# Attention over 2048 batches of 40 fields: one load of x for values and residual of two slots of four, and the shift by the maxima as four 64 by 64 matmuls

## The chip, the cores and the metric

The kernel runs on one core of one Trainium2 chip. The metric is the device time of one execution in microseconds (us); lower is better.

## The reference, cut to what matters

For each of 2048 batches there is x of 40 fields by 64 numbers. Queries, keys, values and a residual are each a projection of x to 128 outputs (4 heads of 32); softmax attention runs over the 40 fields of a batch, per head; the result is relu(attention + residual).

```python
q = (einsum('bfe,oe->bfo', x, Wq) + bq).reshape(B, F, H, D)   # k and v likewise; B=2048 F=40 H=4 D=32
att = einsum('bfhd,bghd->bhfg', q, k) / sqrt(64)
att = softmax(att, axis=-1)
out = einsum('bhfg,bghd->bfhd', att, v).reshape(B, F, H * D)
res = einsum('bfe,oe->bfo', x, Wr) + br
return relu(out + res)
```

## The kernel before

A step handles 8 batches: 4 slots of 2 members. There are 256 steps. Member 0 of a slot lies in partitions 0 to 39 of the working tiles and member 1 in partitions 64 to 103; the lower and the upper 64 rows of TensorE's array are used as separate row groups throughout. `xT` holds x transposed twice, once in partitions 0 to 63 in natural order of the batches, and once in partitions 64 to 127 in the order `ORDER`, in which some slots have their two members exchanged ("crossed").

The order of work on each engine is written out by hand and bound by semaphores. In group n, TensorE does in turn:

- `queries_and_keys(n)` (L382, L386): queries from the lower rows into bank 0 of `o_bank`, keys from the upper rows into bank 1, 320 columns each, float32. A float32 matmul appears in the trace as two passes, each with its own weight load.
- `scores(n-1)` (L402): 16 small matmuls (32 passes, 80 columns) on the four 64 by 64 quarters of the array.
- `attend(n-3)` (L461): 32 small matmuls (64 passes, 33 columns), again on the four quarters. It writes `o_bank`, so it waits until ScalarE (L227) and VectorE (L316) have copied queries and keys out (`copied`).
- `shift(n-2)` (L438): two bf16 matmuls of the full 128 by 128 array and 320 columns that subtract each query's maximum from the scores in `s_buf`: the diagonal matrices `m_diag` made by GpSimd, moved through `pick`, which is nonzero in a 64 by 40 block per member.
- `values_and_residual(n)`: two bias matmuls of 256 columns in bf16 (L419 lower rows, L424 upper rows), and then for each of the four slots one matmul in the lower rows (values, L429) and one in the upper rows (residual, L431), x as the stationary operand and a weight matrix of 128 columns moving. The lower rows write bank 0 of `vr_bank`, the upper rows bank 1.

ScalarE copies `vr_bank` to `rv` (L254), swaps maxima, takes the exponentials of `s_buf` (L247, waits for `shifted`) and the relu (L234). VectorE makes the keys (L316), the maxima (L321, L327 to L332), the reciprocals (L337) and the division (L343), whose `att_ready` lets the next `queries_and_keys` start. GpSimd does three things in each group: `diagonals(n-2)` (L179, needs VectorE's `m_split`), `query_columns(n)` (L195, two instructions) and `add_residual(n-4)` (L187). SyncE's queue loads x eight steps ahead and stores y.

## Time and profile before

| | |
|---|---|
| runs | 938.09 us median of 3 (936.63 to 940.19) |
| the profiled execution | 944.5 us, with a span of 942.4 us |
| granted TensorE clock | 0.995 |
| busy | PE 916.0, PEld 680.3, DVE 726.7, ACT 769.2, POOL 876.5 us |

PE is TensorE's matmuls, PEld its weight loads, DVE VectorE, ACT ScalarE, POOL GpSimd. Times are us from the start of the span unless marked ns. A matmul's start is recorded, its end is modelled and overlaps the next ones, so that a PE that counts as busy may be standing: starts are to be compared with starts. A row of the timeline gives the start of the first of a merged group and the time to the end of its last, so the start of the last is the row's end less the mean duration of one.

### The profile page before, as it was taken

The page shows a single profiled execution, that of the slowest core. Times are in us where ns is not written, and L with a number is a line of the kernel's source. Part 1 is how long each engine was busy: PE and PEld are TensorE (multiplying, and loading weights), DVE is VectorE, ACT ScalarE, POOL GpSimd, SP SyncE. Part 2 cuts the span into 40 slices and gives each one's busy share as a digit, 9 for nine tenths or more (in the row PEclk, how much of TensorE's full clock was granted, in tenths as well). Part 3 has the DMA queues.
Part 4 walks back from the last instruction along what each step waited for, and adds up shares of the span by engine and source line. Part 5 has one row for each costly group of instructions (what it writes and reads, how often), then busy time and mean ns, then how long its engine had stood idle before and what let it go on. Part 6 is the DMA issues. An engine that isn't in the chain of part 4 may idle for free.

```text
span 942.4 us, 68912 instructions
## 1 busy us (share of the span) xinstructions
PE 916.0 (97%) x30720; PEld 680.3 (72%) x30720; DVE 726.7 (77%) x2066; ACT 769.2 (82%) x1541; POOL 876.5 (93%) x1028
## 2 busy tenths in 40 slices
PE   6999999999999999999999999999999999999996
PEld 4777777777777777777777777777777777777774
DVE  6777777778777877777777777777778777777775
ACT  4888888888887888878888788887888888888885
POOL 3999999999998999989999999999999999999997
PEclk9999999999999999999999999999999999999997
DMA  4333333333333333333333333333333333333321
GB/s 117 100 108 109 108 115 110 109 110 115 108 107 105 109 109 108 110 104 107 116 108 110 108 109 114 112 109 102 115 109 109 114 105 116 109 109 106 108 77 65
DMA packets 67433, 101.20 MB, mean 107 GB/s; under 512 B 13632, under 2 KB 46656, under 8 KB 67136
## 3 DMA queue, kind: packets, MB, share of 16 engines
q1 hardware_dynamic: 66704, 96.65, 33.7%
q8 instruction: 239, 3.92, 1.8%
q14 instruction: 58, 0.48, 0.2%
q10 hardware_dynamic: 432, 0.15, 0.1%
HBM read 54.81 MB, written 41.94 MB: 103 GB/s over the span
## 4 chain that ended last, share of the span: by engine, by line
PE 97%; issue 2%; ACT 0%; DMA 0%; DVE 0%; POOL 0%; POOLq 0%; ACTq 0%
PE vr_bank L429 24%; PE o_bank L461 22%; PE s_buf L402 19%; PE o_bank L382 14%; PE s_buf L438 10%; PE vr_bank L419 6%; PE vr_bank L431 1%; DMA biases<-bias_in 0%; PE o_bank L386 0%; POOL y_sum L187 0%; ACT rv L254 0%; ACT y_rows L234 0%; POOLq L35 0%; ACT q_flat L227 0%; PE vr_bank L424 0%
## 5 line engine op out<-in xcount | busy, mean ns | idle before, releaser
L179 POOL TENSOR_TENSOR m_diag<-m_split,ident 128x640 bf16<-128x640 bf16 x256 | 322.2, 1258 | 49.7 <-DVE m_split L332 35.2
L187 POOL TENSOR_TENSOR y_sum<-rv,y_att 128x512 f32<-128x512 f32 x256 | 302.9, 1183 | 1.9 <-DVE y_att L343 1.9
L195 POOL TENSOR_SCALAR q_bd<-q_flat,consts 128x320 f32<-128x320 f32 x512 | 265.8, 532 | 10.8 <-DVE kT L316 10.8
L431 PE MATMUL vr_bank<-w_cols,xT 64*128 64x128 f32 x2048 | 270.9, 273 | 0.0
L429 PE MATMUL vr_bank<-w_cols,xT 64*128 64x128 f32 x2048 | 270.7, 273 | 0.0
L254 ACT ACTIVATE rv<-vr_bank 128x1024 f32<-128x1024 f32 x256 | 260.1, 1016 | 0.0
L321 DVE TRANSPOSE_TENSOR_REDUCE s_buf<-s_buf 128x20 f32<-128x640 f32 x256 | 221.5, 865 | 46.2 <-PE s_buf L402 46.2
L429 PEld LDWEIGHTS vr_bank<-w_cols,xT 64*128 64x128 f32 x2048 | 251.2, 190 | 0.0
L431 PEld LDWEIGHTS vr_bank<-w_cols,xT 64*128 64x128 f32 x2048 | 250.4, 189 | 0.0
L461 PE MATMUL o_bank<-rv,pT 64*40 64x33 f32 x16384 | 225.0, 202 | 10.3 <-issue 8.3
L402 PEld LDWEIGHTS s_buf<-q_bd,kT 64*40 64x40 f32 x8192 | 150.9, 112 | 116.0 <-issue 115.0
L316 DVE TENSOR_SCALAR kT<-o_bank,biases 128x320 f32<-128x320 f32 x256 | 141.0, 551 | 116.7 <-PE o_bank L386 116.7
L461 PEld LDWEIGHTS o_bank<-rv,pT 64*40 64x40 f32 x16384 | 190.3, 118 | 51.8 <-issue 14.6
L227 ACT ACTIVATE q_flat<-o_bank,biases 128x320 f32<-128x320 f32 x256 | 134.9, 527 | 89.9 <-PE o_bank L386 85.6
L402 PE MATMUL s_buf<-q_bd,kT 64*40 64x80 f32 x8192 | 199.9, 233 | 1.2 <-issue 0.5
L247 ACT ACTIVATE pT<-s_buf 128x640 f32<-128x640 f32 x256 | 180.1, 704 | 19.7 <-PE s_buf L438 14.1
L382 PE MATMUL o_bank<-xT,w_cols 64*128 64x320 f32 x512 | 180.6, 433 | 5.7 <-DMA xT<-xT_in 5.7
L343 DVE TENSOR_TENSOR y_att<-o_bank,r_sum 128x512 f32<-128x512 f32 x256 | 177.1, 692 | 9.1 <-DVE r_sum L337 0.3
L386 PE MATMUL o_bank<-xT,w_cols 64*128 64x320 f32 x512 | 180.6, 433 | 0.0
L234 ACT ACTIVATE y_rows<-y_sum 128x512 f32<-128x512 f32 x256 | 159.0, 622 | 2.4 <-POOL y_sum L187 2.4
L240 ACT COPY m_swap<-s_buf 32x20 f32<-32x20 f32 x512 | 85.5, 167 | 54.5 <-DVE s_buf L321 48.4
L438 PE MATMUL s_buf<-m_diag,pick 128*128 128x320 bf16 x512 | 114.2, 305 | 1.1 <-POOL m_diag L179 1.1
(33 smaller groups left out, 624.1 us busy)
## 6 DMA issues: line engine op xcount, KB each, us to landing
xT<-xT_in SPq DMA_DIRECT2D x512, 104.0 KB, 2.5
y<-y_rows SPq DMA_DIRECT2D x512, 80.0 KB
w_cols<-w_in SPq DMA_DIRECT2D x1, 128.0 KB, 2.2
vr_bias<-vr_bias_in ACTq DMA_DIRECT2D x1, 128.0 KB, 3.4
consts<-consts_in ACTq DMA_DIRECT2D x1, 20.0 KB, 2.0
biases<-bias_in ACTq DMA_DIRECT2D x1, 1.0 KB, 3.7
```

What stands on the lines that cost most here:

```text
L179: pool.tensor_tensor(m_diag[:], m_split[:, place % 2].unsqueeze(2).to_broadcast([P, BLOCKS, QUAD]), ident[:].unsqueeze(1).to_broadcast([P, ...
L187: pool.tensor_tensor(y_sum[:, n % 3].rearrange("r (a d) -> r a d", d=DIM), rv[:, place % 4, 1, :, 0:DIM], y_att[:, place % 2].rearrange("r ...
L195: pool.tensor_scalar(q_bd[:, place % 4, :, s], q_flat[:, place % 2].rearrange("d (b f) -> d b f", f=FIELDS), consts[:, C_HEAD + s:C_HEAD + ...
L254: nc.scalar.activation(rv[:, place % 4].rearrange("k t a v -> k (t a) v")[:, :, 0:DIM], vr_bank[:].rearrange("k t (a d) -> k (t a) d", d=DIM),
L321: nc.vector.tensor_reduce(m_part[place % 2].rearrange("k (t b) -> k t b", t=2), s_buf[place % 2][:, :, 0:TOK].rearrange("k t (b c) -> k t ...
L382: nc.tensor.matmul(o_bank[:, 0, 0:TOK], w_cols[0:HALF, 0], tokens(place, 0), start=True, stop=True)
L386: nc.tensor.matmul(o_bank[:, 1, 0:TOK], w_cols[HALF:P, 0], tokens(place, HALF), start=True, stop=True).then_inc(qk_made, 1)
L402: mm = nc.tensor.matmul(s_buf[place % 2][HALF * member:HALF * member + FIELDS, t, 2 * FIELDS * slot:2 * FIELDS * (slot + 1)], kT[rows, pla ...
L429: nc.tensor.matmul(vr_bank[:, 0, OUT * pair:OUT * (pair + 1)], xT[0:HALF, place % 8, cols], w_cols[0:HALF, 1], start=False, stop=True, ski ...
L431: mm = nc.tensor.matmul(vr_bank[:, 1, OUT * pair:OUT * (pair + 1)], xT[HALF:P, place % 8, cols], w_cols[HALF:P, 1], start=False, stop=True ...
L438: mm = nc.tensor.matmul(s_buf[place % 2][:, t, 0:TOK], pick[:].rearrange("k m f -> k (m f)"), m_diag[:, t * (BLOCKS // 2):(t + 1) * (BLOCK ...
L461: mm = nc.tensor.matmul(o_part[HALF * g:HALF * g + FIELDS, member, jj * HEADS + h], pT[HALF * member:HALF * (member + 1), place % 2, h // ...
```

## The change

Three things change in what TensorE does.

1. In `values_and_residual`, slots 0 and 1 are projected as before (values from the lower rows, residual from the upper rows), while slot 2 is loaded once in the lower rows and multiplied by both weight matrices in one matmul of 256 columns, and slot 3 likewise in the upper rows. Values then lie in blocks 0, 1, 2 and 7 of `rv` and residuals in blocks 3 to 6. `w_cols` gets a third matrix (Wr with Wv below it), the column of ones in `rv` is written for all 32 blocks, and the bias goes to blocks 0 and 2 of either half.
2. `shift` becomes four matmuls, one per member and bank half: 64 rows by 40 columns of `pick` as weights, 320 columns moving, each into its member's partitions.
3. In `attend`, the bank of `o_part` follows whether the slot is crossed (slots 0 and 1 now are in both members) in place of the member; the order of the quarters of the array stays.

```diff
--- before.py
+++ after.py
@@ -17,8 +17,12 @@
 PAD = SLOTS * PAIR
 REST = P - PAIR
 
-ORDER = [MEMBERS * slot + member for member in range(MEMBERS) for jj in range(2)
-         for slot in (2 * jj + member, 2 * jj + 1 - member)]
+
+CROSSED = 2
+
+ORDER = [MEMBERS * slot + (member ^ (slot < CROSSED)) for slot in range(SLOTS) for member in range(MEMBERS)]
+
+VALUES, RESIDUAL = (0, 1, 2, 7), 3
 BLOCKS = HEADS * SLOTS * FIELDS // QUAD
 VW = DIM + 1
 SCALE = float(EMB) ** -0.5
@@ -40,7 +44,7 @@
             return ctx.enter_context(nc.semaphore(name))
 
 
-        w_cols = sb("w_cols", [P, 2, OUT])
+        w_cols = sb("w_cols", [P, 3, OUT])
         biases = sb("biases", [P, 2])
         consts = sb("consts", [P, C_ALL])
         pick = sb("pick", [P, MEMBERS, HALF], BF16)
@@ -63,7 +67,7 @@
         q_bd = sb("q_bd", [P, 4, GROUP, 2, FIELDS])
         kT = sb("kT", [P, 4, TOK])
         pT = sb("pT", [P, 2, 2, TOK])
-        rv = sb("rv", [P, 4, 2, SLOTS * HEADS, VW])
+        rv = sb("rv", [P, 4, 2 * SLOTS * HEADS, VW])
         m_swap = sb("m_swap", [P, 2, BLOCKS])
         m_split = sb("m_split", [P, 2, BLOCKS], BF16)
         r_sum = sb("r_sum", [P, 2, 8])
@@ -184,7 +188,7 @@
                 pool.wait_ge(att_ready, n + 1)
                 if not before(n, 3):
                     pool.wait_ge(y_ready, n - 2)
-                pool.tensor_tensor(y_sum[:, n % 3].rearrange("r (a d) -> r a d", d=DIM), rv[:, place % 4, 1, :, 0:DIM],
+                pool.tensor_tensor(y_sum[:, n % 3].rearrange("r (a d) -> r a d", d=DIM), rv[:, place % 4, RESIDUAL * HEADS:(RESIDUAL + SLOTS) * HEADS, 0:DIM],
                                    y_att[:, place % 2].rearrange("r (a d) -> r a d", d=DIM),
                                    ALU.add).then_inc(sum_ready, 1)
 
@@ -217,8 +221,8 @@
             act.dma_start(biases[:], bias_in).then_inc(loaded, 16)
             act.wait_ge(loaded, LOADS)
             for i in range(4):
-                nc.scalar.copy(rv[:, i, 0, :, DIM:VW],
-                               consts[:, C_REAL:C_REAL + 1].unsqueeze(2).to_broadcast([P, SLOTS * HEADS, 1])).then_inc(prepared, 1)
+                nc.scalar.copy(rv[:, i, :, DIM:VW],
+                               consts[:, C_REAL:C_REAL + 1].unsqueeze(2).to_broadcast([P, 2 * SLOTS * HEADS, 1])).then_inc(prepared, 1)
 
             def queries(n, place):
                 act.wait_ge(qk_made, n + 1)
@@ -251,7 +255,7 @@
                 act.wait_ge(vr_made, n + 1)
                 if not before(n, 4):
                     act.wait_ge(sum_ready, n - 3)
-                nc.scalar.activation(rv[:, place % 4].rearrange("k t a v -> k (t a) v")[:, :, 0:DIM],
+                nc.scalar.activation(rv[:, place % 4, :, 0:DIM],
                                      vr_bank[:].rearrange("k t (a d) -> k (t a) d", d=DIM),
                                      ACT.Copy).then_inc(vr_ready, 1)
 
@@ -410,34 +414,45 @@
 
 
 
+                def blocks(half, first, step):
+                    return vr_bank[:, half].rearrange("r (a c) -> r a c", c=OUT)[:, first::step]
+
+                def project(half, pair, first, step, count):
+                    rows = slice(HALF * half, HALF * (half + 1))
+                    return nc.tensor.matmul(blocks(half, first, step)[:, 0:count],
+                                            xT[rows, place % 8, PAIR * pair:PAIR * pair + P],
+                                            w_cols[rows, 1:1 + count],
+                                            start=False, stop=True, skip_group_check=True)
+
                 if not before(n, 1):
                     pe.wait_ge(vr_ready, n)
                 else:
 
                     pe.wait_ge(prepared, PREPARED)
                     pe.wait_ge(set_up, SET_UP)
-                nc.tensor.matmul(vr_bank[:, 0, 0:2 * OUT], bias_pick[0:HALF], bias_rows[0:HALF].rearrange("r s c -> r (s c)"),
+                nc.tensor.matmul(blocks(0, 0, 2), bias_pick[0:HALF], bias_rows[0:HALF],
                                  start=True, stop=False, skip_group_check=True)
                 if exists(n + 1):
 
                     pe.wait_ge(x_loaded[(place + 1) % 8], 32 * turn_of(n + 1, place + 1, 8))
-                nc.tensor.matmul(vr_bank[:, 1].rearrange("r (m j c) -> r m j c", m=MEMBERS, j=2)[:, :, 1],
-                                 bias_pick[HALF:P], bias_rows[HALF:P],
+                nc.tensor.matmul(blocks(1, 0, 2), bias_pick[HALF:P], bias_rows[HALF:P],
                                  start=True, stop=False, skip_group_check=True)
-                for pair in range(SLOTS):
-                    cols = slice(PAIR * pair, PAIR * pair + P)
-                    nc.tensor.matmul(vr_bank[:, 0, OUT * pair:OUT * (pair + 1)], xT[0:HALF, place % 8, cols],
-                                     w_cols[0:HALF, 1], start=False, stop=True, skip_group_check=True)
-                    mm = nc.tensor.matmul(vr_bank[:, 1, OUT * pair:OUT * (pair + 1)], xT[HALF:P, place % 8, cols],
-                                          w_cols[HALF:P, 1], start=False, stop=True, skip_group_check=True)
+                for pair in range(CROSSED):
+                    project(0, pair, pair, 1, 1)
+                    project(1, pair, 1 + pair, 1, 1)
+                project(0, 2, 2, 1, 2)
+                mm = project(1, 3, 0, 3, 2)
                 mm.then_inc(vr_made, 1)
 
             def shift(n, place):
                 pe.wait_ge(diag_ready, n + 1)
                 for t in range(2):
-                    mm = nc.tensor.matmul(s_buf[place % 2][:, t, 0:TOK], pick[:].rearrange("k m f -> k (m f)"),
-                                          m_diag[:, t * (BLOCKS // 2):(t + 1) * (BLOCKS // 2)].rearrange("k b i -> k (b i)"),
-                                          start=False, stop=True, skip_group_check=True)
+                    for member in range(MEMBERS):
+                        rows = slice(HALF * member, HALF * (member + 1))
+                        mm = nc.tensor.matmul(s_buf[place % 2][HALF * member:HALF * member + FIELDS, t, 0:TOK],
+                                              pick[rows, member, 0:FIELDS],
+                                              m_diag[rows, t * (BLOCKS // 2):(t + 1) * (BLOCKS // 2)].rearrange("k b i -> k (b i)"),
+                                              start=False, stop=True, skip_group_check=True)
                 mm.then_inc(shifted, 1)
 
             def attend(n, place):
@@ -451,16 +466,15 @@
                     pe.wait_ge(p_ready, n + 1)
                 if not exists(n + 1):
                     pe.wait_ge(vr_ready, n + 1)
-                for jj in range(2):
+                for idx in range(2):
                     for h in range(HEADS):
-                        for low in range(2):
+                        for c, slot in ((0, CROSSED + idx), (1, idx)):
                             for member in range(MEMBERS):
-                                slot = 2 * jj + low
-                                g = member ^ low
+                                g = member ^ c
                                 at = (2 * slot + h % 2) * FIELDS
-                                mm = nc.tensor.matmul(o_part[HALF * g:HALF * g + FIELDS, member, jj * HEADS + h],
+                                mm = nc.tensor.matmul(o_part[HALF * g:HALF * g + FIELDS, c, idx * HEADS + h],
                                                       pT[HALF * member:HALF * (member + 1), place % 2, h // 2, at:at + FIELDS],
-                                                      rv[HALF * member:HALF * (member + 1), place % 4, 0, slot * HEADS + h],
+                                                      rv[HALF * member:HALF * (member + 1), place % 4, VALUES[slot] * HEADS + h],
                                                       start=True, stop=True, skip_group_check=True)
                 mm.then_inc(o_made, 1)
 
@@ -512,7 +526,8 @@
             xT[:, half, :, :, HALF * member:HALF * member + fields] = columns[:, :, order[member::2]]
     arrays = {
         "xT_in": xT.reshape(steps, P, PAD),
-        "w_in": np.ascontiguousarray(np.stack([np.concatenate([Wq.T, Wk.T]), np.concatenate([Wv.T, Wr.T])], 1)),
+        "w_in": np.ascontiguousarray(np.stack([np.concatenate([Wq.T, Wk.T]), np.concatenate([Wv.T, Wr.T]),
+                                               np.concatenate([Wr.T, Wv.T])], 1)),
         "bias_in": np.ascontiguousarray(np.stack([bq, bk], 1)),
         "vr_bias_in": np.ascontiguousarray(np.stack([bv, br])[None]),
         "consts_in": consts,
@@ -523,9 +538,10 @@
     args.append(nc.dram_tensor("y", (steps, 2, FIELDS, SLOTS * OUT), _mybir.dt.float32, kind="ExternalOutput").ap())
     attention_kernel(nc, *args)
     r = run_bass_kernel_spmd(nc, [arrays], core_ids=[0])
-    rows = r.results[0]["y"].reshape(steps, 2, FIELDS, MEMBERS, 2, OUT)
-    y = np.empty((steps, 2, 2, MEMBERS, FIELDS, OUT), np.float32)
-    for member in range(MEMBERS):
-        for low in range(2):
-            y[:, :, low, member] = rows[:, low ^ member, :, member].transpose(0, 2, 1, 3)
+    rows = r.results[0]["y"].reshape(steps, 2, FIELDS, SLOTS, OUT)
+    y = np.empty((steps, SLOTS, MEMBERS, FIELDS, OUT), np.float32)
+    for slot in range(SLOTS):
+        for member in range(MEMBERS):
+            crossed = slot < CROSSED
+            y[:, slot, member] = rows[:, member ^ crossed, :, slot + 2 if crossed else slot - 2]
     return y.reshape(batch, FIELDS, OUT)
```

## Rows read from the trace of the kernel before

**Rows 1.** The page, busy time of each engine

```profile
PE 916.0 (97%) x30720; PEld 680.3 (72%) x30720; DVE 726.7 (77%) x2066; ACT 769.2 (82%) x1541; POOL 876.5 (93%) x1028
```

**Rows 2.** The page, the chain that ended last, by engine

```profile
PE 97%; issue 2%; ACT 0%; DMA 0%; DVE 0%; POOL 0%; POOLq 0%; ACTq 0%
```

**Rows 3.** Timeline of one step: start, length, engine, line, count

```profile
316.38 0.43 PE L382 MATMUL o_bank<-xT,w_cols 64*128 64x320 f32 x1
...
316.49 1.26 POOL L179 TENSOR_TENSOR m_diag<-m_split,ident 128x640 bf16<-128x640 bf16 x1
316.74 0.76 PE L402 MATMUL s_buf<-q_bd,kT 64*40 64x80 f32 x32
...
316.86 0.55 DVE L316 TENSOR_SCALAR kT<-o_bank,biases 128x320 f32<-128x320 f32 x1 [0.45 <-PE o_bank L386]
...
317.47 0.82 PE L461 MATMUL o_bank<-rv,pT 64*40 64x33 f32 x64
...
318.22 0.45 PE L438 MATMUL s_buf<-m_diag,pick 128*128 128x320 bf16 x2
...
318.60 0.28 PE L419 MATMUL vr_bank<-bias_rows,bias_pick 64*128 64x256 bf16 x1
...
318.64 0.69 DVE L343 TENSOR_TENSOR y_att<-o_bank,r_sum 128x512 f32<-128x512 f32 x1
...
319.61 0.43 PE L382 MATMUL o_bank<-xT,w_cols 64*128 64x320 f32 x1
```

**Rows 4.** Timeline: the last passes of values and residual, then queries

```profile
319.39 0.27 PE L429 MATMUL vr_bank<-w_cols,xT 64*128 64x128 f32 x1
...
319.50 0.27 PE L429 MATMUL vr_bank<-w_cols,xT 64*128 64x128 f32 x1
...
319.88 0.43 PE L382 MATMUL o_bank<-xT,w_cols 64*128 64x320 f32 x1
```

**Rows 5.** The page, costliest groups: busy us, mean ns of one, idle before

```profile
L179 POOL TENSOR_TENSOR m_diag<-m_split,ident 128x640 bf16<-128x640 bf16 x256 | 322.2, 1258 | 49.7 <-DVE m_split L332 35.2
L187 POOL TENSOR_TENSOR y_sum<-rv,y_att 128x512 f32<-128x512 f32 x256 | 302.9, 1183 | 1.9 <-DVE y_att L343 1.9
L195 POOL TENSOR_SCALAR q_bd<-q_flat,consts 128x320 f32<-128x320 f32 x512 | 265.8, 532 | 10.8 <-DVE kT L316 10.8
...
L461 PE MATMUL o_bank<-rv,pT 64*40 64x33 f32 x16384 | 225.0, 202 | 10.3 <-issue 8.3
...
L402 PE MATMUL s_buf<-q_bd,kT 64*40 64x80 f32 x8192 | 199.9, 233 | 1.2 <-issue 0.5
...
L438 PE MATMUL s_buf<-m_diag,pick 128*128 128x320 bf16 x512 | 114.2, 305 | 1.1 <-POOL m_diag L179 1.1
```

**Rows 6.** Source view of the first bias matmul's weight load: duration, first and last start

```profile
L419 PEld LDWEIGHTS vr_bank<-bias_rows,bias_pick x256: 92/93/102, 8.5 to 927.2; 64*128 64x128 bf16 x128
```

**Rows 7.** Timeline of TensorE, three longer steps: the second piece of attend

```profile
284.02 0.76 PE L461 MATMUL o_bank<-rv,pT 64*40 64x33 f32 x58 [0.16 <-issue]
...
288.04 0.69 PE L461 MATMUL o_bank<-rv,pT 64*40 64x33 f32 x50 [0.22 <-issue]
...
292.06 0.61 PE L461 MATMUL o_bank<-rv,pT 64*40 64x33 f32 x42 [0.22 <-issue]
```

**Rows 8.** The page, DMA queues: packets, MB

```profile
q8 instruction: 239, 3.92, 1.8%
```

**Rows 9.** Timeline of GpSimd alone over one step

```profile
320.00 1.26 POOL L179 TENSOR_TENSOR m_diag<-m_split,ident 128x640 bf16<-128x640 bf16 x1
321.24 1.04 POOL L195 TENSOR_SCALAR q_bd<-q_flat,consts 128x320 f32<-128x320 f32 x2
322.24 1.19 POOL L187 TENSOR_TENSOR y_sum<-rv,y_att 128x512 f32<-128x512 f32 x1
323.50 1.26 POOL L179 TENSOR_TENSOR m_diag<-m_split,ident 128x640 bf16<-128x640 bf16 x1
```

**Rows 10.** Timeline of the first 14 us

```profile
8.54 0.37 PE L419 MATMUL vr_bank<-bias_rows,bias_pick 64*128 64x256 bf16 x1 [1.37 <-DVE pick L310]
```

## The prediction

> **What bounds the kernel now.** I read the page's busy times first: TensorE and GpSimd are both above 90% [rows 1]. The chain that ended last lies on TensorE for nearly all of the span [rows 2]. But a matmul's end is modelled, so the chain cannot say whether TensorE works or stands. For that I took one step of the timeline and compared starts [rows 3]. From queries to queries it is cut so:
>
> - second queries pass 316.38 to first score 316.74: 0.36 us, of which the 320 columns take 0.27 (the same two passes are 0.27 apart in [rows 4]). Some 0.09 us are a gap, where the array goes from 64-row, 128-column tiles to 64 by 40 ones.
> - scores, 316.74 to 317.47: 0.73. Attend starts 0.06 us after VectorE has ended its copy of the keys (316.86 + 0.55 = 317.41). So this piece is the wait for the copies; the last score started at 317.50 less 0.23 [rows 5], that is 317.27.
> - attend, 317.47 to 318.22: 0.75. Its last pass started at 318.29 less 0.20 [rows 5] = 318.09, and shift starts 0.13 later. A pass of 33 columns needs, at the 0.83 ns a column of the queries (0.27 us for 320), 0.03. Again 0.10 us of gap, here from 64 by 40 tiles to the full array.
> - shift, 318.22 to 318.60: 0.38. Its second matmul started at 318.67 less 0.305 [rows 5] = 318.36, so one takes 0.14, two take 0.28, and 0.10 is a gap again, from the full array to 64 by 128.
> - bias, values and residual, 318.60 to 319.61: 1.01.
>
> With the 0.27 between the two queries passes this is 3.50 us, all of it TensorE's order and one wait on the copies. The mean step is longer: the first bias loads run from 8.5 to 927.2 over 255 steps [rows 6], 3.60 each. The 0.10 of difference is not spread evenly: in a long step attend falls into two pieces, with 0.16 to 0.22 us of standing between them, by the modelled ends, that no semaphore explains [rows 7]. There are 61440 loads and matmuls [rows 1] in 239 packets of instructions [rows 8], 257 to a packet against 240 to a step; in three such steps 58, 50 and 42 passes stand behind the break [rows 7], 8 passes or 16 instructions fewer a step, as the border of a packet would move. I take these breaks for late instruction packets: about 255 x 0.10 = 26 us in all.
>
> The second engine matters as much. GpSimd's step is 1.24 from diagonals to query columns, 1.00 on to the residual sum, and 1.19 for that sum [rows 9]; neighbours on GpSimd overlap by 0.02 to 0.04 in the records. That is 3.43 less 0.04, so 3.39 us when nothing holds it. Its busy time gives 876.5 / 256 = 3.42 [rows 1], less that last overlap the same 3.39. GpSimd has 0.11 us of slack in a step of 3.50, no more.
>
> **The change part by part.**
>
> Shift. The two switches of shape around it become one: attend's quarters and the new shift's are the same 64 by 64 tiles, so the 0.10 gap between attend and shift [rows 3] should go. That such a gap is not there without a switch is seen between scores and attend only in part, since the copies cover it. I price it at 0.10; bounds are 0 (the gap belongs to the end of attend, whatever follows) and 0.12 (the whole distance from the last attend pass but 0.01). The gap before the bias matmuls stays, since a switch remains. The streaming itself: four matmuls of 320 columns in two pairs, each pair on two different quarters (lower rows to lower partitions, upper rows to upper partitions). If a pair runs at once it takes 0.14 and two take 0.28, as now. That quarters do run at once is in the scores: 32 passes whose first and last start are 0.53 us apart (316.74 to 317.27), 0.017 a pass, where one pass of 80 columns streams 0.067. That is four at a time. I take 0.28; the other bound is 4 x 0.14 = 0.56, that is 0.28 us a step more. The four weight loads of 40 columns instead of two of 128 lie under attend's last passes and under the first pair, and cost nothing; uncovered, the nearest load row is 93 ns [rows 6] once.
>
> In all that the trace shows, lower and upper rows never write one bank together: queries and keys, scores, attend and values all keep one row group to one bank. The new shift is the first place where a pair writes the same bank, in different partitions. Here the Trainium skill speaks against the change: TensorEngine Tiling (Array Packing), Gotcha 1: PSUM Pressure, says that different row tiles cannot access the same PSUM bank simultaneously. Its page PSUM — Partial Sum Buffer, section PSUM bank collisions raise a hardware error, narrows this: different column tiles may share a bank if their partitions are disjoint, which holds here. By the first the sum is that of the second rival below; by the second that of the forecast. No row of before shows the case.
>
> Values and residual. The columns are the same: 2 x 128 + 256 in each half in place of 4 x 128. A pass of 128 columns takes 0.111 (319.39, 319.50, 319.61), one of 320 takes 0.27 [rows 3, 4]; on the line between them 256 takes 0.217, against 0.222 for two of 128. Two float32 passes: 0.01 us a step saved. That two weight loads a step go away in each half saves nothing by itself, because the passes are already as long as their columns on that line; bounds 0 and 0.02. The bias matmuls keep 256 columns: 0.
>
> Attend. The same 64 passes on the same quarters in the same order, other banks: within a group of four, neighbours now share a bank in different partitions. I price it at 0, on the same ground as shift; the upper bound is attend at half its overlap, 0.75 more, which would go with the second rival.
>
> Around it. ScalarE's copy of `vr_bank` and GpSimd's sum keep their sizes. The division sends `att_ready` at about 319.33 + 0.06 = 319.39, and the next queries start at 319.61: 0.22 of cover, of which the change takes 0.11, so that wait stays hidden. `m_diag` is done at 316.49 + 1.26 = 317.75 and wanted at 318.22, then 0.10 earlier: hidden too, until GpSimd falls behind. The 64 KB more of weights and the wider column of ones lie before 8.54, where TensorE has waited 1.37 us for VectorE's bias [rows 10]: 0.
>
> **The sum.** TensorE: 3.50 - 0.10 - 0.01 = 3.39 a step. GpSimd: 3.39. They meet, so a gain beyond 0.11 cannot show. The breaks for instruction packets stay as they are, 236 instructions a step against 240. I take 0.105 a step for two engines so close together: 256 x 0.105 = 27 us. The profiled execution goes from a span of 942.4 to 915.5 and from 944.5 to 917.6; it lies 6.4 us above the median of the runs, and 938.09 - 27 = **911 us**.
>
> **The rivals.**
>
> 1. Forecast, 911: chance 0.70, own range 904 to 920 (the breaks may go by a third, 9 us, either way).
> 2. Pairs of the shift run one after the other, because two row groups write one bank. For it: no row shows such a pair at once, and every stage before keeps its row groups in banks of their own. Against: the partitions are disjoint, and quarters run four at a time in the scores. The tiling page of the Trainium skill, cited above, speaks for this rival. Price +0.28 - 0.11 = +0.17 a step, 44 us: 982 us, slower. It decides from the point where the second of a pair starts more than 0.055 us after the first (two pairs eat 0.11). Chance 0.12.
> 3. The change does little: the gap ahead of shift is attend's own tail and stays. Then only 0.01 a step, 3 us: 935; with half of the gap, 922. For it: attend's ends are modelled, and each gap in the trace stands at a change of stage as well as of shape. Against: the gap is 0.09 to 0.10 at three switches behind matmuls of 320, 33 and 320 columns alike. The Trainium skill, in TensorEngine Tiling (Array Packing), Key Properties, says that changing the tiling mode, and not merely the tile, drains the engine; by it the time is the forecast's. Chance 0.11, of which 0.03 at half.
> 4. The breaks in attend grow, as the same instructions are wanted in less time and the shift's loads and matmuls, four more instructions, stand right behind attend. A break of 0.3 in every third step instead of the present mean of 0.10 would be half again, +13 us: 924. Chance 0.07, of which 0.01 within 0.5% of before.
>
> A measurement of this kernel can tell about 0.5%, some 5 us. Faster by more: 0.70 + 0.06 + 0.03 = 0.79. Within: 0.08 + 0.01 = 0.09. Slower: 0.12. The range leaves out the second rival and little else: 903 to 936.
>
> **What would show it.** In a quiet step: shift starts under 0.05 us after the last attend pass, not 0.13; the two matmuls of a shift pair start together and the pairs 0.13 to 0.14 apart; from shift's start to the bias still 0.38; the 256-column passes 0.217 apart; the step 3.39 and GpSimd with no idle time before its diagonals. Wrong would be: shift pairs staggered by 0.13 (second rival), the gap ahead of shift still there (third), attend longer than 0.65 to its last start, or GpSimd's step above 3.39, with shift waiting on `m_diag`.

## The result, and the profile after

The changed kernel takes 924.84 us (median of 4 runs, 921.35 to 926.6) against 938.58 us before (median of 4): a ratio of 0.985, 95% interval [0.9814, 0.9886]. It is faster by 13.7 us where 27 were forecast. The interval leaves out 1, so the gain is real, though it is under 2%. A second comparison (run c0 below) gave 0.9846 [0.9826, 0.9866].

The profiled execution took 923.84 us with a span of 921.1. The page of the changed kernel, busy times, then the chain that ended last by engine, then the queue of TensorE's instructions:

```profile
PE 892.3 (97%) x30208; PEld 626.7 (68%) x30208; DVE 726.7 (79%) x2066; ACT 770.6 (84%) x1541; POOL 872.1 (95%) x1028
...
PE 93%; POOL 3%; issue 2%; DVE 1%; DMA 0%; ACT 0%; POOLq 0%; ACTq 0%
```

```profile
q8 instruction: 235, 3.85, 1.8%
```

236 loads and matmuls a step (60416 / 256) in place of 240, and GpSimd and VectorE now have pieces of the chain, where [rows 2] had none. One quiet step in the timeline answers to [rows 3]:

```profile
352.57 0.45 PE L386 MATMUL o_bank<-xT,w_cols 64*128 64x320 f32 x1
...
352.86 0.43 PE L386 MATMUL o_bank<-xT,w_cols 64*128 64x320 f32 x1
...
353.10 1.26 POOL L183 TENSOR_TENSOR m_diag<-m_split,ident 128x640 bf16<-128x640 bf16 x1
353.22 0.76 PE L406 MATMUL s_buf<-q_bd,kT 64*40 64x80 f32 x32
...
353.95 0.82 PE L475 MATMUL o_bank<-rv,pT 64*40 64x33 f32 x64
...
354.58 0.44 PE L452 MATMUL s_buf<-m_diag,pick 64*40 64x320 bf16 x4
...
354.95 0.28 PE L433 MATMUL vr_bank<-bias_rows,bias_pick 64*128 64x256 bf16 x1
...
355.07 1.04 PE L422 MATMUL vr_bank<-w_cols,xT 64*128 64x128 f32 x12
355.12 0.69 DVE L347 TENSOR_TENSOR y_att<-o_bank,r_sum 128x512 f32<-128x512 f32 x1
...
355.95 0.45 PE L386 MATMUL o_bank<-xT,w_cols 64*128 64x320 f32 x1
```

By starts: attend to shift 0.63 in place of 0.75, and the last attend pass (354.77 less 0.20 = 354.57) stands 0.01 ahead of the shift, not 0.13. Shift to bias 0.37, bias to queries 1.00 in place of 1.01. Together with 0.65 and 0.73 for the first two pieces this is 3.38 us, against 3.50. One thing is new: the first queries pass takes 0.29 instead of 0.27. Another step shows the shift's pairs at once:

```profile
319.31 0.32 PE L452 MATMUL s_buf<-m_diag,pick 64*40 64x320 bf16 x2
319.34 0.21 PE L475 MATMUL o_bank<-rv,pT 64*40 64x33 f32 x2
319.45 0.32 PE L452 MATMUL s_buf<-m_diag,pick 64*40 64x320 bf16 x2
```

The two matmuls of a pair are one row of the timeline, the next pair follows 0.14 later, and the shift starts while attend's last passes are still going in. GpSimd alone:

```profile
349.70 1.27 POOL L183 TENSOR_TENSOR m_diag<-m_split,ident 128x640 bf16<-128x640 bf16 x1
...
353.10 1.26 POOL L183 TENSOR_TENSOR m_diag<-m_split,ident 128x640 bf16<-128x640 bf16 x1
...
356.47 1.27 POOL L183 TENSOR_TENSOR m_diag<-m_split,ident 128x640 bf16<-128x640 bf16 x1
```

3.40 and 3.37 apart: GpSimd runs without idle time here. In the whole trace 135 of its steps have no idle time, and they take 3.384 us at the median. The first of the next two rows, from the view of waits (us in total, times, longest), is one that the kernel before did not have at all, the queries' weight load waiting for the division. The second says that GpSimd still waits for VectorE 91 times, as it did 92 times before:

```profile
PEld o_bank L386 <- DVE y_att L347: 35.4, 214, 0.3
POOL m_diag L183 <- DVE m_split L336: 30.1, 91, 1.6
```

So a quiet step came out as forecast. The mean step did not. The first bias loads (source view, to be read as [rows 6]) give (906.5 - 8.7) / 255 = 3.52, and the long steps are there as before, with the break in attend:

```profile
L433 PEld LDWEIGHTS vr_bank<-bias_rows,bias_pick x256: 92/92/99, 8.7 to 906.5; 64*128 64x128 bf16 x128
```

```profile
326.65 0.46 PE L475 MATMUL o_bank<-rv,pT 64*40 64x33 f32 x26 [0.33 <-issue]
```

### The profile page after: what moved, and what is told of

Read it like the earlier page. It is cut to its first block, busy times and chain, and to the rows that moved or that the text cites. A ratio compares the mean times of both kernels' runs of the same rounds, so it can differ in the third digit from the quotient of the medians.

```text
span 921.1 us, 67888 instructions
## 1 busy us (share of the span) xinstructions
PE 892.3 (97%) x30208; PEld 626.7 (68%) x30208; DVE 726.7 (79%) x2066; ACT 770.6 (84%) x1541; POOL 872.1 (95%) x1028
## 3 DMA queue, kind: packets, MB, share of 16 engines
q8 instruction: 235, 3.85, 1.8%
## 4 chain that ended last, share of the span: by engine, by line
PE 93%; POOL 3%; issue 2%; DVE 1%; DMA 0%; ACT 0%; POOLq 0%; ACTq 0%
PE vr_bank L422 24%; PE o_bank L475 22%; PE s_buf L406 19%; PE o_bank L386 15%; PE s_buf L452 7%; PE vr_bank L433 6%; POOL y_sum L191 1%; POOL m_diag L183 1%; POOL q_bd L199 1%; PE o_bank L390 0%; DMA biases<-bias_in 0%; ACT y_rows L238 0%; POOLq L39 0%; DVE s_buf L325 0%; PE vr_bank L438 0%
## 5 line engine op out<-in xcount | busy, mean ns | idle before, releaser
L422 PE MATMUL vr_bank<-w_cols,xT 64*128 64x128 f32 (+1 forms) x3072 | 269.0, 308 | 0.1
L475 PE MATMUL o_bank<-rv,pT 64*40 64x33 f32 x16384 | 229.6, 202 | 12.1 <-issue 8.4
L475 PEld LDWEIGHTS o_bank<-rv,pT 64*40 64x40 f32 x16384 | 192.9, 117 | 54.4 <-issue 17.9
L422 PEld LDWEIGHTS vr_bank<-w_cols,xT 64*128 64x128 f32 x3072 | 195.2, 190 | 0.2 <-issue 0.2
L386 PE MATMUL o_bank<-xT,w_cols 64*128 64x320 f32 x512 | 186.8, 445 | 5.7 <-DMA xT<-xT_in 5.7
L390 PE MATMUL o_bank<-xT,w_cols 64*128 64x320 f32 x512 | 187.5, 446 | 0.0
L452 PE MATMUL s_buf<-m_diag,pick 64*40 64x320 bf16 x1024 | 114.9, 297 | 2.0 <-POOL m_diag L183 1.6
L386 PEld LDWEIGHTS o_bank<-xT,w_cols 64*128 64x128 f32 x512 | 76.6, 186 | 45.7 <-DVE y_att L347 35.4
L336 DVE TENSOR_TENSOR m_split<-s_buf,m_split 32x20 bf16<-32x20 f32 x512 | 88.5, 173 | 16.6
```

Of the source, the lines that this page charges most:

```text
L386: nc.tensor.matmul(o_bank[:, 0, 0:TOK], w_cols[0:HALF, 0], tokens(place, 0), start=True, stop=True)
L390: nc.tensor.matmul(o_bank[:, 1, 0:TOK], w_cols[HALF:P, 0], tokens(place, HALF), start=True, stop=True).then_inc(qk_made, 1)
L422: return nc.tensor.matmul(blocks(half, first, step)[:, 0:count], xT[rows, place % 8, PAIR * pair:PAIR * pair + P], w_cols[rows, 1:1 + coun ...
L452: mm = nc.tensor.matmul(s_buf[place % 2][HALF * member:HALF * member + FIELDS, t, 0:TOK], pick[rows, member, 0:FIELDS], m_diag[rows, t * ( ...
L475: mm = nc.tensor.matmul(o_part[HALF * g:HALF * g + FIELDS, c, idx * HEADS + h], pT[HALF * member:HALF * (member + 1), place % 2, h // 2, a ...
```

## The experiments

All numbers of steps in this table come from the starts of the first queries matmul in each of the last 250 groups of TensorE's timeline. A step counts as quiet if it is within 0.06 us of the fastest fiftieth; the quiet column is the mean of those, "long" the number of the others, "breaks" the mean step less the quiet one. "Packet" is the time that 256 instructions take at the quiet pace, quiet x 256 / N, with N the loads and matmuls of a step. Ratios are to the kernel before on the same chip, which took 941.6 us beside c0 to e3, 942.1 beside e4 to e7 and 936.8 beside e8 to e11 (medians). Where e4 to e11 are set against c0, two ratios from different chips are subtracted, so a difference is known to some 3 or 4 us only.

| kernel | N | quiet | long | breaks | mean step | packet | ratio, 95% |
|---|---|---|---|---|---|---|---|
| before | 240 | 3.502 | 92 | 0.098 | 3.601 | 3.74 | 1 |
| changed | 236 | 3.387 | 117 | 0.131 | 3.518 | 3.67 | 0.985 [0.9814, 0.9886] |
| c0, changed again | 236 | 3.386 | 122 | 0.151 | 3.537 | 3.67 | 0.9846 [0.9826, 0.9866] |
| e1, shift only | 244 | 3.395 | 155 | 0.194 | 3.589 | 3.56 | 1.0058 [1.0032, 1.0083] |
| e2, projection only | 232 | 3.487 | 52 | 0.055 | 3.542 | 3.85 | 0.9878 [0.9857, 0.9898] |
| e3, one more switch | 234 | 3.474 | 74 | 0.080 | 3.554 | 3.80 | 0.988 [0.9858, 0.9902] |
| e4, half division | 236 | 3.370 | 103 | 0.137 | 3.507 | 3.66 | 0.9791 [0.9768, 0.9813] |
| e5, short sum | 236 | 3.385 | 104 | 0.119 | 3.505 | 3.67 | 0.9803 [0.9777, 0.9829] |
| e6, both | 236 | 3.370 | 98 | 0.137 | 3.507 | 3.66 | 0.9815 [0.9792, 0.9838] |
| e7, 256 instructions | 256 | 3.466 | 213 | 0.356 | 3.823 | 3.47 | 1.0584 [1.0559, 1.0609] |
| e8, the same, moved | 256 | 3.468 | 160 | 0.257 | 3.726 | 3.47 | 1.0416 [1.0371, 1.0461] |
| e9, four more | 240 | 3.393 | 114 | 0.152 | 3.545 | 3.62 | 0.9913 [0.9879, 0.9946] |
| e10, light stores | 236 | 3.387 | 86 | 0.107 | 3.494 | 3.67 | 0.9733 [0.9695, 0.9772] |
| e11, no bias | 233 | 3.385 | 124 | 0.127 | 3.513 | 3.72 | 0.9838 [0.9795, 0.9881] |

In e11 the profile lists 232 loads and matmuls a step, but its breaks keep one place in the packet only if 233 instructions a step are counted. That the further one is a wait, since two waits now stand ahead of one matmul, is inferred from the edit.

**c0 and the two parts.** c0 is the changed kernel unedited. e1 is the kernel before with one edit:

```diff
-                    mm = nc.tensor.matmul(s_buf[place % 2][:, t, 0:TOK], pick[:].rearrange("k m f -> k (m f)"), ...)
+                    for member in range(MEMBERS):
+                        rows = slice(HALF * member, HALF * (member + 1))
+                        mm = nc.tensor.matmul(s_buf[place % 2][HALF * member:HALF * member + FIELDS, t, 0:TOK],
+                                              pick[rows, member, 0:FIELDS], ...)
```

e2 is the changed kernel with that edit undone.

> The changed kernel once more, on the chip on which its parts run. Theory A (the time of a step is what its starts show: 3.41 us in a quiet step in place of 3.50, and breaks for instruction packets that vary from execution to execution): ratio 0.98 to 0.99, a spread of some 5 us. Theory B (the first ratio was too small by chance, and the gain is the 21 us between the two profiled spans): 0.975 to 0.98.

> The kernel before with only the shift changed. Theory A (the gap ahead of shift is the change of the array's shape): attend's start to shift's start 0.64 in place of 0.75, queries 0.66 in place of 0.63 because they now wait for the division, projection unchanged at 1.01; step 3.42, ratio about 0.987, nearly all of the change's gain. Rival (the gain comes from the fewer loads of the projection, or from the banks of attend): step above 3.48, ratio above 0.995.

> The changed kernel with the old shift of two full matmuls, so the new projection and attend's new banks alone. Theory A: projection 1.00 in place of 1.01, attend to shift 0.75 as before, step 3.49, ratio 0.995 to 1.00. Rival (fewer loads matter): ratio below 0.993.

c0's ratio was that of theory A, which puts the smaller gain of the first comparison down to more than chance. The stages of the two parts were as expected: e1's attend to shift 0.64 and its quiet step 3.395, e2's projection 1.00 and its quiet step 3.487. The times were the other way about: the shift alone, which brings 0.107 us a quiet step, made the kernel 0.6% slower, and the projection alone, which brings 0.015, made it 1.2% faster. What changed with them is the number of instructions (244 and 232) and with it the breaks. The view of waits for e1, then for e2, attend's loads that waited for nothing the profile shows:

```profile
PEld o_bank L464 <- issue: 24.9, 73, 1.1
```

```profile
PEld o_bank L472 <- issue: 7.8, 23, 1.1
```

My theory A had the ratios of both wrong: it priced the step by its quiet form. "Fewer loads matter", the rival for e2, was right in its number and not in its place: the projection became only 0.01 shorter.

**Is the gap the switch of shape?** e3 does the shift's first half in quarters and its second half as one full matmul.

```diff
-                for t in range(2):
-                    for member in range(MEMBERS):
...
+                for member in range(MEMBERS):
+                    ... (t = 0, as in the changed kernel)
+                mm = nc.tensor.matmul(s_buf[place % 2][:, 1, 0:TOK], pick[:].rearrange("k m f -> k (m f)"), ...)
```

> The changed kernel in which the shift's first half is done in quarters and the second half by one matmul of the full array: the same columns, one more change of shape, in the middle of the shift. Theory A (each change of shape costs 0.10 us): shift to bias 0.47 in place of 0.37, attend to shift still 0.64, step 3.48 to 3.50, ratio about 1.00. Rival (the gap is attend's tail, whatever follows, and four matmuls merely hide it): shift to bias stays at 0.37 to 0.39 and the time that of the changed kernel.

Timeline of e3:

```profile
400.92 0.82 PE L477 MATMUL o_bank<-rv,pT 64*40 64x33 f32 x64
401.56 0.30 PE L451 MATMUL s_buf<-m_diag,pick 64*40 64x320 bf16 x2
401.79 0.31 PE L455 MATMUL s_buf<-m_diag,pick 128*128 128x320 bf16 x1
402.03 0.28 PE L433 MATMUL vr_bank<-bias_rows,bias_pick 64*128 64x256 bf16 x1
```

The pair of quarters starts 0.64 after attend's start, as in the changed kernel, and the full matmul 0.23 after the pair, where a second pair came 0.14 after: 0.09 for the switch. Shift to bias is 0.47. So the gap is the price of a change of the array's shape, each time, and not attend's tail. The ratio of theory A, about 1.00, was wrong again: the time rose by only 3.5 us over c0, because the breaks fell from 0.151 to 0.080 while the quiet step rose by 0.088, two instructions fewer in a longer step.

**Who holds the quiet step now?** e4 divides only half of the attention output (c = 0), e5 sums only 384 of 512 columns on GpSimd, e6 does both.

```diff
-                nc.vector.tensor_tensor(y_att[:, place % 2].rearrange("r (c a d) -> r c a d", c=2, d=DIM), o_part[:, :, :, 0:DIM], ...
+                nc.vector.tensor_tensor(y_att[:, place % 2, 0:2 * OUT].rearrange("r (a d) -> r a d", d=DIM), o_part[:, 0, :, 0:DIM], ...
```

```diff
-                pool.tensor_tensor(y_sum[:, n % 3].rearrange("r (a d) -> r a d", d=DIM), ...
+                pool.tensor_tensor(y_sum[:, n % 3, 0:3 * OUT].rearrange("r (a d) -> r a d", d=DIM), ...
```

> The changed kernel with a division of only the first half of the attention output (256 of 512 columns; the rest of y_att stays zero), so that VectorE lets the queries start some 0.3 us earlier. Theory A (the changed kernel's queries wait for the division, which was covered before): queries' start to scores' start back from 0.66 to 0.63, quiet step 3.39, now GpSimd's; 5 to 7 us less than the changed kernel. Rival (GpSimd alone holds the step): quiet step unchanged at 3.38 to 3.41, time the same within 2 us.

> The changed kernel with GpSimd adding the residual to only three quarters of the columns (384 of 512; the rest of y_sum stays zero), 0.3 us less on GpSimd in each step. Theory A (the division holds the queries, GpSimd close behind): time within 3 us of the changed kernel, GpSimd with idle time before its diagonals. Rival (GpSimd holds the step): quiet step at TensorE's own 3.38, 5 us or more less.

> Both of these at once (half of the division and three quarters of the sum left in). Theory A: TensorE alone is left, quiet step 0.63 + 0.73 + 0.64 + 0.37 + 1.00 = 3.37 us, some 8 to 10 us less than the changed kernel, the rest of the distance to the forecast being breaks for instruction packets. Rival (the step is held by neither): as the changed kernel.

e4 did as theory A said in the stage and the time: queries to scores back at a median of 0.63, and a ratio 0.0055 below c0's, 5 us. Its quiet step became 3.370, and not the 3.39 of theory A. By the quiet step alone the wait for the division costs 0.016 x 256 = 4 us. e5's quiet step stayed at 3.385, with GpSimd now idle in every step, so it is the division that holds it. Its ratio is 0.0043 below c0's, 4 us, between the two expectations; its long steps are fewer, 104 against 122. e6 has e4's quiet step and no more gain than either alone, where 8 to 10 us were expected: with the quiet step at TensorE's own 3.37, GpSimd is not what keeps the mean at 3.507; the breaks, 0.137 a step, are.

**The breaks.** In the kernel before, I counted the loads and matmuls from the start of the program to each break in attend: all 40 places inside attend where two neighbouring matmuls start more than 0.2 us apart stand at 188 modulo 256, the border of a packet. In the changed kernel it is 76 of 77. e7 adds 10 tiny matmuls a step behind the scores, where TensorE waits for the copies anyway, which makes 256 instructions a step and fixes the border's place.

```diff
+                if before(n, 4):
+                    return
+                for i in range(PADS + (EXTRA if n == 4 else 0)):
+                    rows = slice(HALF * (i % 2), HALF * (i % 2) + HALF)
+                    nc.tensor.matmul(s_buf[(place + 1) % 2][HALF * (i % 2):HALF * (i % 2) + 33, 1, 500:501],
+                                     pick[rows, 0, 0:33], pick[rows, 0, 0:1], start=False, stop=True, ...)
```

PADS is 10 and EXTRA 0 in e7; 10 and 45 in e8; 2 and 0 in e9.

> The changed kernel with 10 tiny bf16 matmuls (64 by 33, one column, into an unused column of s_buf) after the scores of each step, where TensorE stands and waits for the copies. A step then has 256 loads and matmuls, and a border between instruction packets always lies at the same place, in the projection. Theory A (the breaks are late instruction packets, and show only where instructions are short): no breaks in attend, all steps 3.38 to 3.45, 20 to 30 us less than the changed kernel. Rival (the breaks have another cause, or the padding costs what it saves): breaks as before, time the same or longer.

Both were wrong on the size. Timeline of e7:

```profile
421.73 0.39 PE L430 MATMUL vr_bank<-w_cols,xT 64*128 64x128 f32 x4
422.51 0.93 PE L430 MATMUL vr_bank<-w_cols,xT 64*128 64x128 f32 x8 [0.40 <-issue]
423.17 0.43 PE L387 MATMUL o_bank<-xT,w_cols 64*128 64x320 f32 x1
423.28 0.43 PE L391 MATMUL o_bank<-xT,w_cols 64*128 64x320 f32 x1
...
425.75 0.39 PE L430 MATMUL vr_bank<-w_cols,xT 64*128 64x128 f32 x4
426.53 0.93 PE L430 MATMUL vr_bank<-w_cols,xT 64*128 64x128 f32 x8 [0.40 <-issue]
```

The border lies where the count puts it, after 4 of the 12 projection passes, and attend has no break. But the break now stands in the projection, in 213 of 250 steps, and the kernel is 5.8% slower. A slow stage does not hide a late packet. My theory A ("breaks show only where instructions are short") fell. In its place theory C: a packet of 256 instructions takes about 3.8 us to come, so that mean step / N is the bound. Until then, N divided by the mean step had been 65.5 to 68 instructions a us in every kernel. Four runs to try it (the kernel that e8's expectation starts from is e7); e10 and e11 have these edits:

```diff
-                sp.dma_start(out[n, g], y_rows[HALF * g:HALF * g + FIELDS, place % 4]).then_inc(y_stored[place % 4], 16)
+                sp.dma_start(out[n, g, 0:8], y_rows[HALF * g:HALF * g + 8, place % 4]).then_inc(y_stored[place % 4], 16)
```

```diff
-                nc.tensor.matmul(blocks(0, 0, 2), bias_pick[0:HALF], bias_rows[0:HALF], start=True, stop=False, ...)
-                nc.tensor.matmul(blocks(1, 0, 2), bias_pick[HALF:P], bias_rows[HALF:P], start=True, stop=False, ...)
-                    project(0, pair, pair, 1, 1)
-                    project(1, pair, 1 + pair, 1, 1)
+                    project(0, pair, pair, 1, 1, start=pair == 0)
+                    project(1, pair, 1 + pair, 1, 1, start=pair == 0)
```

> As the kernel before this one (256 loads and matmuls to a step), but with 45 more tiny matmuls once, in the fifth step, which moves the border between packets from the projection into the middle of attend. Theory C (a packet of 256 instructions takes some 3.8 us to come, and TensorE cannot run through them faster, wherever the border lies): mean step 3.80 to 3.84, time within 3 us of it. Theory A (a break costs where the instructions are short): attend broken in every step and a time that differs by 10 us or more.

> The changed kernel with 2 tiny matmuls (4 instructions) a step after the scores, where TensorE stands anyway: 240 instructions a step as in the kernel before. Theory C (the time goes with the number of instructions): mean step 3.57 to 3.60, 12 to 18 us over the changed kernel, ratio 0.998 to 1.005, though every quiet step stays at 3.38 to 3.41. Rival (two tiny matmuls cost what they take in their place): within 4 us of the changed kernel, ratio 0.983 to 0.988.

> The changed kernel that stores only 8 of each 40 rows of y (the others stay unwritten), so that the stores bring a fifth of their packets and bytes. Theory C1 (instruction packets queue behind the kernel's own transfers in the DMA engines): breaks shrink, mean step 3.40 to 3.45, 15 to 28 us less than the changed kernel. Theory C2 (the instruction stream has its own pace): time within 4 us of the changed kernel.

> The changed kernel without the two bias matmuls (the output lacks bv and br): 232 instructions a step, TensorE's own order 0.12 us shorter, so that the quiet step is GpSimd's and the division's 3.38. Theory C: mean step 3.44 to 3.47, 13 to 20 us less than the changed kernel, because four instructions are gone. Rival (breaks cost 0.12 to 0.13 a step as before, and the quiet step is held at 3.38): mean step 3.50, at most 6 us less.

e8, timeline of one step: the border is in attend, with 34 passes and one more behind it, again as counted.

```profile
449.38 0.50 PE L483 MATMUL o_bank<-rv,pT 64*40 64x33 f32 x29
450.29 0.53 PE L483 MATMUL o_bank<-rv,pT 64*40 64x33 f32 x34 [0.42 <-issue]
```

Its time is not e7's: ratio 1.0416 against 1.0584, mean step 3.726 against 3.823. e9 came out 0.0067 over c0, 6 us, between theory C's 12 to 18 and the rival's 4. e11 gained nothing that can be measured over c0 (0.9838 against 0.9846), where theory C wanted 13 to 20 us; that is what its rival said. So a fixed pace for the instruction stream, too, is not the law: theory C fell in that form. e10 gained 0.0113 (some 0.004 either way), 10.6 us, under the 15 expected of C1 but clear of C2's 4; the page shows what was taken away from the transfers, here the data queue of c0, then the data queue and the instruction queue of e10:

```profile
q1 hardware_dynamic: 66704, 96.72, 34.8%
...
q1 hardware_dynamic: 49296, 63.16, 24.9%
q8 instruction: 235, 3.85, 1.8%
```

What stands across the fourteen profiles is weaker and safer: the less time 256 instructions take at the quiet pace, the larger the breaks. 3.80 to 3.85 us goes with 0.055 to 0.080 a step, 3.72 to 3.74 with 0.098 to 0.127, 3.66 to 3.67 with 0.107 to 0.151, 3.62 with 0.152, 3.56 with 0.194, 3.47 with 0.257 to 0.356. From 3.85 to 3.56 that is 0.14 us of breaks for 0.29 us: half of what a shorter step gives is taken back. Two profiles of one program (changed and c0) differ by 0.020, so small differences in this list mean nothing.

**When a packet lands.** The traces also record each packet's own transfer, on queue q8, and they say more than the counts. In all fourteen, exactly one packet lands between two borders (in e11 when 233 are counted). No border, after the first few, is crossed less than 1.18 us after its packet has landed, whatever the kernel. The breaks inside attend stand at that wall: their matmul starts 1.19 to 1.70 us after the landing, at a median of 1.40 to 1.47. In the break of e8 shown above the packet came in from 447.72 to 448.68, and the matmul behind the border started at 450.29, 1.61 later. So a break is TensorE waiting for a packet.

A packet is late because it sets out late and travels long. At the median of each kernel it starts 1.0 to 1.3 us after the border before it has been crossed; in none of the fourteen do more than 4% start ahead of that border. It then takes 0.88 us at least and 1.97 at most, and the part behind the landing follows. Ahead of a break in attend the transfer takes 1.14 to 1.24 us at the median, ahead of an unbroken border in attend 0.96 to 1.02. From border to landing it is 2.42 to 2.55 us ahead of a break and 2.00 to 2.16 otherwise. With 1.40 to 1.47 behind the landing, a late packet's way is 3.8 to 4.0 us, and with the least of 1.2 a quick one's is 3.2 to 3.4 (estimates, sums of these medians). The quiet pace wants 256 instructions in 3.47 to 3.85 us, between the two. So theory C's 3.8 us is the slow side of a spread and not a fixed pace, and the shorter the time wanted, the more packets fall behind it.

## Why the prediction was right, and where it was not

**The sign and the range** were right: 924.8 lies between 903 and 936, and faster had 0.79. The number was 14 us too low, and the gain half of the forecast. The range reached to within 3 us of no change at all, so lying inside it says little; the stages say more.

**The terms of the quiet step** were right. Shift: 0.10 forecast, 0.107 in e1. Projection: 0.01 forecast, 0.015 in e2. Pairs of the shift at once in one bank, in different partitions: shown, the two starts of a pair 0.007 us apart and 0.14 between pairs; the second rival is out, and with it, for this case, the rule of the Trainium skill's page TensorEngine Tiling (Array Packing), Gotcha 1: PSUM Pressure, as it stands there. The Trainium skill's page PSUM — Partial Sum Buffer, section PSUM bank collisions raise a hardware error, repeats that rule for row tiles, which the prediction did not say; what it states of column tiles with disjoint partitions agrees with the trace. The third rival is out by e3: 0.09 more for one switch more. GpSimd's floor of 3.39 was where I put it (3.384, and 3.377 in e4), but e5 shows that the quiet step of the changed kernel is held by the division and not by GpSimd. The sum, 3.39, was measured as 3.387: 0.115 x 256 = 29 us.

**The step that failed** is "the breaks for instruction packets stay as they are". They grew from 0.098 a step to 0.131, 8 us, between the two profiled executions. The rest of the distance is in the base: the profiled execution of before took 944.5 us, 5.9 over the median of its 4 runs, that of the changed kernel 1.0 under its own. So the spans differ by 21.3 us and the medians by 13.7 (20.7 - 5.9 - 1.0 = 13.8). If those 5.9 and 1.0 us are breaks too, which only profiles of more executions could show, a usual execution has breaks of about 0.075 before and 0.135 after, and 29 less 15 is the 14 us measured. The fourth rival named this mechanism and came to 13 us more of breaks and 924 us. That its number fits is partly luck: a break of 0.3 in every third step, as it says, is a mean of 0.10 and so no increase at all; 13 us need 0.05 a step more. I gave it 0.07, since I had read the breaks as a toll per packet and not as something that depends on how soon the next packet is wanted. The rows to see it were there: breaks came in runs of steps, and in the quiet stretches between them the border was outside attend, so that the packet after it was wanted later. Of 122 steps with the border in attend 76 were long, of 31 with the border in the projection one.

**A smaller miss** was "that wait stays hidden". I counted 0.22 us of cover between `att_ready` and the queries' start; the queries' first weight loads wait behind the same signal, and before they had started together with the projection's last pass. 214 of 256 times they now waited, the first pass grew by 0.02, and e4 prices it at 4 to 5 us. One reading was wrong without effect: the wait in [rows 10] is for `pick`, not for VectorE's bias.

**What is shown and what stays open.** That a break is a late packet is shown: its place follows the count in two kernels built for it (e7, e8), and it ends a near constant time after the packet's landing. Why a packet sets out only about 1.1 us after the border, and why TensorE needs 1.2 us more behind the landing, no run tells. That the kernel's own transfers have a share is shown by e10, at about 11 us of the 34 to 39 (0.131 and 0.151 x 256) that breaks cost the changed kernel in two profiles. Its packets take 1.10 us on average against 1.15 in c0. Why e7 and e8 differ by 1.7% is not explained.

## What to carry to other kernels

Where TensorE executes hundreds of small matmuls a step, count its instructions along with its time: here a change that took 0.107 us from every quiet step at four instructions more lost time, and one that took 0.015 and eight instructions won 1.2%. Price a change by the mean step and not by the quiet one, and ask what the same instructions in less time do to their supply: in these traces the way of a packet could last 4.0 us, and every kernel wanted 256 instructions sooner than that. And where a signal has cover left, count the weight loads that stand behind it too.

## What the runs showed of the hardware

- A change of the array's shape costs 0.09 to 0.10 us here, whichever shapes they are (three places before, one more in e3), and nothing where the shape stays: shift's first pair starts 0.01 after attend's last pass. At a change the first weight load of the new shape starts only together with its matmul, 0.13 us after attend's last pass in the kernel before; in the changed kernel it starts 0.03 ahead of the shift's first matmul.
- A packet of 256 instructions moves in 0.88 to 1.97 us here, one lands between two borders, and TensorE crosses no border sooner than 1.18 us after the landing (fourteen traces).
- In e7 and e8 the length of a step lies on a ladder: 3.47, 3.75, 4.02 us, with the break at a fixed instruction. A late packet costs a multiple of about 0.27 us there.
- In e7, where the border lies in the projection in each step, the lower and upper row groups stay out of step. The queries of the lower rows start at 423.17 and those of the upper rows at 423.28, and queries to scores takes 0.74 in place of 0.63 in nearly every step, unbroken ones too, although the two have no data in common. Single steps of other kernels show such a lag of over 0.05 (4 of the changed kernel, 19 of e1), each time with the last border in the projection; the kernel before, with 31 borders there, has none. What decides it is not shown.
